# The attention stage of a four-layer graph network: plain distances by two products of 512 columns, and no products of zeros

## The reference, cut to what matters

```python
h = (node_features @ W + b).reshape(N, 4, 32)
s_i = jnp.einsum('nhf,hf->nh', h, a_i);  s_j = jnp.einsum('nhf,hf->nh', h, a_j)
eij = jax.nn.leaky_relu(s_i[tgt] + s_j[src], negative_slope=0.2)
m = jax.ops.segment_max(eij, tgt, num_segments=N)
ex = jnp.exp(eij - m[tgt])
denom = jax.ops.segment_sum(ex, tgt, num_segments=N)
out = jax.ops.segment_sum((ex / denom[tgt])[:, :, None] * h[src], tgt, num_segments=N) + h
```

## Time and profile before

| | |
|---|---|
| time of three runs, median (lowest to highest) | 12574.69 us (12566.58 to 12575.17) |
| profiled execution, first to last instruction (span) | 15198.0 us |
| instructions recorded | 174858 |
| PE busy | 7352.3 us (48%) |
| PE weight loads busy | 5826.6 us (38%) |
| DVE busy | 5571.9 us (37%) |
| ACT busy | 2825.4 us (19%) |
| POOL busy | 8278.1 us (54%) |

### The profile page before, as it was taken

One profiled execution on the slowest core, in us unless ns is written; L12 is line 12 of the kernel. 1 busy time (PEld: TensorE's weight loads), 2 busy tenths in 40 slices (PEclk: granted clock), 3 DMA queues, 4 the chain that ended last, 5 costly groups with the idle time before them and its releaser, 6 DMA issues. The chain is left out here.

```text
span 15198.0 us, 174858 instructions
## 1 busy us (share of the span) xinstructions
PE 7352.3 (48%) x42682; PEld 5826.6 (38%) x42906; DVE 5571.9 (37%) x10022; ACT 2825.4 (19%) x7817; POOL 8278.1 (54%) x8916
## 2 busy tenths in 40 slices
PE   7444444463323324333333886777777773333332
PEld 4343333332222223333232764555555553222222
DVE  5444444431111113212111886655555654111111
ACT  4000000020000002111111004555555553000000
POOL 1555656626666664666666124444444444666665
PEclk8666666676565666556666997777777776565565
DMA  4111111141111111111111761111111111222222
GB/s 179 40 40 40 40 40 40 42 156 45 45 45 45 45 45 51 43 44 43 43 44 43 187 150 45 38 38 38 38 38 38 39 38 49 47 47 47 47 47 58
DMA packets 628740, 846.66 MB, mean 56 GB/s; under 512 B 167762, under 2 KB 464219, under 8 KB 628212
## 3 DMA queue, kind: packets, MB, share of 16 engines
q0 software_dynamic: 270448, 573.37, 14.6%
q1 hardware_dynamic: 225848, 205.13, 4.3%
q10 hardware_dynamic: 131916, 62.14, 1.6%
HBM read 598.43 MB, written 244.10 MB: 55 GB/s over the span
## 5 line engine op out<-in xcount | busy, mean ns | idle before, releaser
L1206 POOL DMA_INDIRECT GF<-TAB,IDXA x3322 | 3212.3, 967 | 2220.4 <-issue 1197.2
L1250 PE MATMUL PSUM<-GF,OH 128*128 x10560 | 2292.5, 401 | 4035.2 <-SPq L1191 2396.1
L1250 PEld LDWEIGHTS PSUM<-GF,OH 128*128 128x128 f32 x10560 | 2095.4, 302 | 4213.9 <-issue 4213.3
L1774 POOL DMA_INDIRECT GF<-HTAB,IDS x1760 | 1678.9, 954 | 1754.4 <-PE PSUM L1951 1015.8
L1123 DVE TENSOR_TENSOR OH<-PSUM,DLOA 128x1024 f32<-128x1024 f32 x660 | 804.4, 1222 | 4346.5 <-remote 1927.9
L1533 POOL DMA_INDIRECT MSG<-GF,IDS x1661 | 1610.5, 970 | 1072.7 <-ACT GF L1463 584.1
L1206 POOL DMA_INDIRECT GF<-HROW,IDXA x1661 | 1570.9, 946 | 949.3 <-issue 475.6
L1521 PE MATMUL PSUM<-ACC,SCR 128*128 x3520 | 736.5, 388 | 1198.4 <-ACT PSUM L1441 1029.4
L2031 DVE TENSOR_REDUCE SM<-PSUM 128x8 f32<-128x1024 f32 x880 | 1074.7, 1221 | 311.4 <-remote 208.0
L1521 PEld LDWEIGHTS PSUM<-ACC,SCR 128*128 128x128 f32 x3520 | 675.9, 289 | 1234.1 <-issue 1234.0
L1489 DVE CAST SCR<-PSUM 128x1024 f32<-128x1024 bf16 x220 | 269.4, 1225 | 2043.1 <-remote 1551.7
(11 more groups left out here) (388 smaller groups left out, 10841.7 us busy)
## 6 DMA issues: line engine op xcount, KB each, us to landing
GF<-MSG ACTq DMA_DIRECT2D x880, 66.0 KB, 2.2
GF<-MSG SPq DMA_DIRECT2D x880, 66.0 KB, 2.2
GF<-TAB,IDXA POOLq DMA_INDIRECT x3322
TAB<-SCR SPq DMA_DIRECT2D x100, 512.0 KB, 2.6
TAB<-OH SPq DMA_DIRECT2D x96, 512.0 KB, 2.6
GF<-HTAB,IDS POOLq DMA_INDIRECT x1760
MSG<-GF,IDS POOLq DMA_INDIRECT x1661
GF<-HROW,IDXA POOLq DMA_INDIRECT x1661
```

Source lines behind the costliest of these rows:

```text
L1206: q.indirect_dma_start(G[:, t % RING, k, 0:row], None, table, bass.IndirectOffsetOnAxis(ap=IDXA[:, at:at + 1], axis=0)).then_inc(s_got[t % ...
L1250: m = q.matmul(PSUM[:, bass.ds(places[k], w)], OH[:, r % 2, k, :], GW[:, bass.ds(rows[k], w)], start=False, stop=False, skip_group_check=True)
L1774: q.indirect_dma_start(GT[:, r, k, :], None, HTAB, bass.IndirectOffsetOnAxis(ap=IDS[:, r, k:k + 1], axis=0)).then_inc(s_got[r], 16)
```

## The change

The plain distances of a group, before eight products of 128 columns with the same weights, become two products of 512 columns; the moving operand is the same MSEL, read as four of its eight planes at a time, and the banks are the same two. Both loops of products of zeros go, with the constant BUSY and the waits that only they had: for ROWS of the next group in `scores` and for the cleared sums in `plain`. `main` has a wait for the cleared sums of its own, and pair 0 of the next group waits for its ROWS earlier in PE's order.

```diff
-        BUSY = (8, 6)
...
                         wait(q, s_z, 3 * (x - 1) + 3)
-                        if there(x + 1):
-                            q.wait_ge(s_sj, x + 2)
-                            for _ in range(BUSY[0]):
-                                q.matmul(PS[7][:, 0:256], ZERO[:, 0:P], ZERO[:, 0:256], start=True, stop=True)
                         q.wait_ge(s_ot, x + 1)
...
-                        if d and there(x - d) and not (isinstance(x, int) and x < d):
-                            q.wait_ge(s_cl, x - d + 1)
-                            for _ in range(BUSY[1]):
-                                q.matmul(PS[4][:, 0:3 * RW], ZERO[:, 0:P], ZERO[:, 0:3 * RW], start=False, stop=False, skip_group_check=True)
                         q.wait_ge(s_red, PAIRS * x + 3)
-                        for k in range(K):
-                            m = q.matmul(BANKS[0][:, k * P:(k + 1) * P], ROWS[rx % 2][:, 0:P], MSEL[:, k, :], start=True, stop=True)
+                        for half in range(2):
+                            m = q.matmul(PS[half], ROWS[rx % 2][:, 0:P], MSEL[:, half * PAIRS:(half + 1) * PAIRS, :].rearrange("p k n -> p (k n)"),
+                                         start=True, stop=True)
                         m.then_inc(s_hm, 1)
```

## The result

The changed kernel takes 12979.99 us (median of four runs, 12964.48 to 12993.41), the kernel before 12572.74 (four runs, 12566.58 to 12575.17): a ratio of 1.0322, 95% interval 1.031 to 1.0334. It is slower by 407 us. The forecast was 12825, slower by 252.

A forecast was written before the change was run, and what follows sets the result against it. A chain from engine to engine paced the attention stage, 15.5 us a group. Terms of +1.15 us a group, times 219, made +252 us; 12574.69 + 252 was given as 12825 us, with an 8-in-10 range of 12515 to 13060.

The forecast's parts named there:

- The mechanism: On PE ahead of plain: without zeros PE stands still for 1.4 us, so its clock rises during main, not before.
- main would run low altogether: By the skill's rule main stays at the lower clock, the high end of its term, up to 1.56 us lost.
- The clock term: On PE: main, turned and scores take 0.9, 0.2 and 0.25 us a group longer as the clock rises later.
- The direct gain of 0.2 us a group: Ahead of plain: removing zeros gives 0.30 us at the low clock, nothing at the high; 0.2 taken as mean.
- Plain's own term: Plain's batch at the lower clock: up to 0.15 us a group lost, taken as 0.
- The sum: Attention stage: -0.2 + 0.9 + 0.2 + 0.25 = +1.15 us a group, times 219 = +252 us.
- the likeliest case: Clock rising later: 12650 to 13030 us, 0.3 to 2.1 us a group slower; chance 0.54.
- the recorder stretches something: Whole program: timed 12574.69 us is 0.827 of the profiled span, laid to the recorder; added array time not scaled.
- B: DVE's wait after scores swallows the loss if fetches set it: 12575 us, give or take 25; chance 0.12.
- D: DVE's wait after scores is a backlog zeros help build, shrinking by half of 664.1 us: 12240 us; chance 0.05.
- The marks: Seven signs in the profile after, among them main about 3.2 us, scores about 2.3, granted clock under 0.7.

The follow-up runs named there:

- plain loads: Eight indirect fetches of each attention group replaced by one plain load, gather left out, in both kernels: kernel before 14200.88 us, changed kernel 14610.88 us.
- wide version: Kernel before with two-product plain, six zeros ahead of plain kept, four of 512 columns ahead of scores instead of eight of 256: 14842.09 us, ratio 0.9852.
- plain alone: Kernel before with plain in two products of 512 columns, both loops of zeros kept: 14976.93 us against 15090.53, ratio 0.9926.
- changed kernel's repeated profile: The changed kernel run again unchanged, against the kernel before in the same batch: 15160.89 us against 15162.93, ratio 0.9997.

## Why the prediction was right, and where it was not

- **The mechanism held.** Zeros gone, PE pauses ahead of plain, and the clock rises later than before. It rises later even than forecast, behind main and not inside it: the opened group after has 0.50 through plain and main, and 132 of the 220 batches of main take 3.6 to 3.8 us, 37 under 2.1. The Trainium skill ("TensorE: Matmul & The Clock Gate", Part 1) states that activity releases the throttle. The trace agrees, for the opened group, with what the prediction drew from it, that main would run low altogether; over the stage the mean of 3.33 us lies between the 3.17 of the forecast and the 3.83 of the lower level.
- **The clock term was mis-sized, and so was its base.** I took main, scores and turned from their means in the stage of before, 2.27, 2.07 and 0.61 us, and added 0.9, 0.25 and 0.2. The level after was forecast well: about 3.2 for main (3.33 measured) and 2.3 for scores (2.36). But with plain loads, before is at 2.07 and 2.01: its clock is 0.97, not 0.76, and so main loses 1.20 us and scores 0.36. Turned loses 0.05, less than the 0.2 assumed.
- **The direct gain of 0.2 us a group did not exist.** It was read where the zeros ahead of plain ran at the lower clock. With plain loads they run at the upper one and end early: there PE's idle time ahead of plain that the maximum ends is 177.3 us in all, 0.8 us a group. I had written that the gain is nothing at the high clock, and then chose the mean of a mixture that the measured runs did not have.
- **Plain's own term was set to 0** and came to 0.22 us a group (135.9 against 184.9 us), because it too fell to the lower clock. The form, two products or eight, costs nothing beside zeros: the stage of the wide version with plain loads is as long as before's, and plain alone with the fetches had 0.9926. Without zeros the two forms were run only with fetches and on different chips, eight products at 0.9903 and two at 0.9997, so that a cost of the form there is not ruled out.
- **The sum.** In the pair with plain loads the terms are 1.20 + 0.36 + 0.05 + 0.22 = 1.83 us a group, 402 us over 220 groups, against 410 measured; the prediction had 1.15. All but turned were too small, and the result is 1.6 times the forecast slowdown. A slip besides: 0.3 us a group is 12640, not 12650, as the lower end of the likeliest case.
- **The step that was wrong is "the recorder stretches something".** The profile was of another condition. Its late starts of z, 2.7 us a group, which I kept as they were, are absent at 12.6 ms, and where they are present the change shortens them. For the condition that the profile showed, the forecast of +252 would have been wrong: the ratio there is 0.9997. That the timed runs came from the condition without them was luck. Rivals B and D, which I gave 0.17 between them, come near that condition: the time is B's, no change, and the shrinking wait is D's. D priced the shrinking at 332 us; it was 304, but main and scores took 280 us more and the late starts elsewhere grew by 312, so that D's faster kernel did not come of it. D was dismissed with the last groups, which have the zeros and no wait. That only showed that fetches are needed for the wait as well.
- **The marks.** Main and scores rose as stated; the granted clock, 0.70, missed "under 0.7" narrowly, and the rise is not inside main; plain starts behind the maximum as stated, and its batch, 1.03 us at the lower clock, is as before. Scores start 0.34 us after TURN in the opened group, and at the median of all, where 0.24 was stated; why it is 0.1 us more was not looked into. The last mark, wrong altogether if the stage is not over 3417 us, was drawn on the wrong condition: the stage is 2887 us, and the kernel is slower all the same.

Open: what the two conditions are. Four chips were in the 15.1 ms one in every run, with every variant, and the stages outside attention are stretched as well: 9217 us stand ahead of the attention stage in the changed kernel's repeated profile and 7900 in its first. The chip of the result's runs is not on record, so that it is not shown whether the condition belongs to a chip. What makes DVE and ACT start late behind a batch of PE products while indirect fetches run was not tried, nor why eight zeros ahead of scores move the lateness to z.

## What to carry to other kernels

When the span of a profile and the timed runs differ by a fifth, do not blame the recorder: ask which waits of the profile would have to vanish to give the timed figure, and forecast for both. Products of zeros in pauses were worth 3% of the whole program here, whose attention stage has its chain over PE. Products of 8 columns did not hold the clock, and four of 512 ahead of scores did as well as eight of 256: try few and wide ones. Before taking an effect off the list because it is absent in one stretch, check what else is absent in that stretch. And when a wait shrinks, look for another that has grown before calling the difference a gain.

## What the runs showed of the hardware

- With plain loads, two loops of zeros in pauses of about 1.1 and 2.3 us go with a granted clock of 0.97 over the stage; without them it is 0.72. Main's batch, sixteen records of fp32 products of 132 columns, takes 3.73 us in the group opened after the change, and 2.06 with the clock at its upper level.
- In the 15.1 ms condition, DVE starts z up to 7.6 us after PE's last product of scores when indirect fetches run beside it, in place of 0.06 on average without the condition or without the fetches. Late starts of DVE and ACT behind PE batches add up to 899 to 1010 us in the stage of all eight kernels with fetches, whatever their zeros. On z fall 439 to 589 us of them with eight products queued ahead of scores, 187 to 289 with four or none.
- The same change had ratios of 1.0322 and 0.9997 in the two conditions, each with an interval of about 0.1% either way. A ratio between two kernels is no safer from the condition it is taken in than a time.
